# Layer 0's experts: the square root of a sum of squares on ScalarE instead of a power on GpSimd

## The reference, cut to what matters

```python
V = x @ Wv.T + bv                                   # after a layer norm of x
r = Vf @ Wg.T + bg                                  # [tokens, 8]
pv = einsum('epd,nd->nep', Wp, Vf)                  # [tokens, 8 experts, 8 projections]
c = sqrt(sum(pv * pv, axis=-1)) / sqrt(8)           # [tokens, 8]
s = _ln(r, g_r, b_r) + sigmoid(alpha) * _ln(c, g_c, b_c)
topv, sel = top_k(s, 2)
w = softmax(topv, axis=-1)
for e in range(8):
    h = silu(Vf @ W1[e].T + b1[e])
    out = h @ W2[e].T + b2[e]
    we = sum(where(sel == e, w, 0.0), axis=-1)
    delta = delta + out * we[:, None]
return Vf + delta                                   # added to x
```

## Time and profile before

| | before |
|---|---|
| median of 3 runs | 1920.31 us (1911.11 to 1921.92) |
| profiled execution | 1911.35 us |
| its span, first to last instruction | 1909.3 us |
| mean granted TensorE clock | 0.935 of 2.4 GHz |
| busy: PE / DVE / ACT / POOL | 1602.4 / 1267.7 / 1025.7 / 791.0 us |
| table loads on ACT | 13 |
| chain that ended last | PE 58%, DVE 20%, ACT 11%, POOL 6% |

### The profile page before, as it was taken

How to read it: one execution, slowest core, us unless ns; L and a number is a source line. 1 busy time by engine, 2 the same in 40 slices (tenths; PEclk the granted TensorE clock), 3 DMA queues, 4 the chain that set the end, 5 groups by cost and what they waited for, 6 DMA issues and landing times.

```text
span 1909.3 us, 29013 instructions
## 1 busy us (share of the span) xinstructions
PE 1602.4 (84%) x10660; PEld 920.5 (48%) x10660; DVE 1267.7 (66%) x2849; ACT 1025.7 (54%) x1967; POOL 791.0 (41%) x734
## 2 busy tenths in 40 slices
PE   6789899867988898987787889996778898999867
PEld 3456664313545676521354567651235456754214
DVE  4655558998554464799865455589975545549995
ACT  4555446655555444665455544466545554455654
POOL 2331215885132112588614220268841422117791
PEclk9999999888999998988899999998789999999789
DMA  6004402020000440212000053021100014302110
GB/s 220 1 1 137 133 16 73 28 89 12 12 1 1 141 134 11 73 40 78 12 12 1 4 162 113 14 71 59 55 12 6 1 40 135 111 18 77 49 46 12
DMA packets 91982, 105.41 MB, mean 55 GB/s; under 512 B 7104, under 2 KB 70336, under 8 KB 91584
## 3 DMA queue, kind: packets, MB, share of 16 engines
q1 hardware_dynamic: 89792, 99.37, 16.9%
q0 software_dynamic: 2048, 4.20, 0.7%
HBM read 80.60 MB, written 22.94 MB: 54 GB/s over the span
## 4 chain that ended last, share of the span: by engine, by line
PE 58%; DVE 20%; ACT 11%; POOL 6%; issue 4%; DMA 1%; DVEq 0%; SPq 0%; ACTq 0%; POOLq 0%
PE P L238 12%; DVE M L2038 7%; PE P L1652 6%; PE P L1881 4%; POOL M L2108 3%; PE P L1233 2%; PE P L406 2%; PE P L978 2%; PE P L2166 2%; DVE st L185 2%; PE P L1238 2%; PE P L1249 2%; DVE M L200 1%; PE P L1660 1%; PE P L1205 1%
## 5 line engine op out<-in xcount | busy, mean ns | idle before, releaser
L2038 DVE TENSOR_TENSOR_SCAN M<-P,M 128x512 f32<-128x512 f32 x384 | 444.9, 1204 | 19.5 <-ACT P L1973 17.8
L1973 ACT ACTIVATE P<-M,negA 128x512 f32<-128x512 f32 x384 | 262.3, 689 | 170.5 <-DVE M L2038 167.9
L1881 PE MATMUL P<-M,wt 32*32 32x512 f32 x3072 | 247.0, 712 | 105.4 <-DVE M L2038 64.3
L238 PEld LDWEIGHTS P<-wt,M 128*128 128x128 f32 x2176 | 278.2, 194 | 100.5 <-issue 43.9
L238 PE MATMUL P<-wt,M 128*128 128x128 f32 x2176 | 292.1, 280 | 10.0 <-ACT M L1980 4.0
L2108 POOL TENSOR_TENSOR M<-M 128x512 f32<-128x512 f32 x192 | 238.6, 1273 | 104.6 <-ACT M L1955 75.0
L2108 POOL TENSOR_TENSOR M<-W,M 128x512 f32<-128x512 f32 x192 | 242.9, 1294 | 62.9 <-PE P L1881 62.8
L1881 PEld LDWEIGHTS P<-M,wt 32*32 32x32 f32 x3072 | 38.9, 111 | 251.1 <-DVE M L2038 156.0
L1749 DVE TENSOR_TENSOR M<-M,P 128x512 f32<-128x512 f32 x128 | 87.0, 682 | 76.7 <-PE P L1660 72.5
L1652 PE MATMUL P<-M,wt 128*128 128x512 f32 x256 | 134.5, 607 | 0.8 <-ACT M L1701 0.5
L1701 ACT ACTIVATE M<-P 128x512 f32<-128x512 f32 x128 | 76.4, 597 | 101.2 <-PE P L1652 92.9
(11 more groups left out here) (352 smaller groups left out, 3225.9 us busy)
## 6 DMA issues: line engine op xcount, KB each, us to landing
W<-in_e SPq DMA_DIRECT2D x88, 192.0 KB, 2.7
M<-in_e SPq DMA_DIRECT2D x64, 192.0 KB, 2.6
M<-dt SPq DMA_DIRECT2D x48, 256.0 KB, 4.4
M<-xs SPq DMA_DIRECT2D x32, 256.0 KB, 3.2
ys<-M SPq DMA_DIRECT2D x32, 256.0 KB, 2.3
W<-du SPq DMA_DIRECT2D x32, 256.0 KB, 4.8
W<-xh SPq DMA_DIRECT2D x16, 256.0 KB
M<-du SPq DMA_DIRECT2D x16, 256.0 KB, 4.2
```

The lines of the kernel that those rows point to most:

```text
L238: m = e.matmul(out[:, tok(j)], h[:, tok(j)], wgt, start=first and j == 0, stop=last, skip_group_check=True)
L1881: m = e.matmul(t["sums"][i // 2][to:to + 32, :], part("WC", c)[r, r], scan[r, :], start=c == 0, stop=c == 5, tile_position=(32 * i, to))
L1973: e.activation(t["aa"][n % 2][:, :], t["dtr"][i][:, :], EXP, scale=negA[:, c:c + 1]).then_inc(ACT.s, ACT.mark(b, "a3", "aa", n))
L2038: e.tensor_tensor_scan(bb[:, :], t["aa"][n % 2][:, :], bb[:, :], 0.0, MUL, ADD).then_inc(DVE.s, DVE.mark(b, "a3", "scan", n))
```

## The change

ScalarE's own square root, with its scale of 1/8 applied to the input, takes the place of VectorE's multiplication and GpSimd's power. It stands in ScalarE's queue after the square and ahead of the hidden layer's identity and tanh. The sums now wait in `sm[:, 72:104]` for ScalarE and the roots go to the same place as before, `sm[:, 40:72]`; VectorE's next step waits for ScalarE instead of GpSimd.

```diff
+    SQRT = ACTF.Sqrt
@@ act_ffn0
                 ACT.s, ACT.mark(b, "f0", "sq"))
+            yield
+            w.wait_ge(DVE.s, DVE.of(b, "f0", "c0"))
+            e.activation(sm[:, 40:72], sm[:, 72:104], SQRT, scale=0.125).then_inc(ACT.s, ACT.mark(b, "f0", "c"))
             for c in range(2):
@@ dve_ffn0
                 DVE.s, DVE.mark(b, "f0", "c0"))
-            yield
-            w.wait_ge(DVE.s, DVE.of(b, "f0", "c0"))
-            e.tensor_scalar(sm[:, 72:104], sm[:, 72:104], 0.125, None, MUL).then_inc(DVE.s, DVE.mark(b, "f0", "c1"))
@@ dve_ffn0
-            w.wait_ge(POOL.s, POOL.of(b, "f0", "c"))
+            w.wait_ge(ACT.s, ACT.of(b, "f0", "c"))
@@ pool_ffn0
-            yield
-            w.wait_ge(DVE.s, DVE.of(b, "f0", "c1"))
-            e.tensor_tensor(sm[:, 40:72], sm[:, 72:104], wv("phalf"), POW).then_inc(POOL.s, POOL.mark(b, "f0", "c"))
@@ TURNS
-            "scalar": (1644,
-                "002400333318e7ff69df001089009bb2fe7f7b44217503374ae88087d9884491949249a4a040244adfaffbfffffdb6f76961"
+            "scalar": (1652,
+                "0000600da71a39ffb4edb002224026d9bebb3111adee052dcee68101f662451412a2495511021112b7f3fffbfffedb7eb4aa"
...
```

More of the change, by code:

```diff
@@ L2266, in program @@
             "tensor": (2211,
[L2267 to L2270, removed]
@@ L2271, in program @@
-                "0b584c95ff07b201b33e800366436ffc2d77fffe07f0800001089840ef0c70ffe237bb3ccd140f7fe10fe1be136e80000000"
-                "3cf003e1ed519feeeeeefdddee87a576ac12bffffff08f8506dfe"),
-            "scalar": (1644,
-                "002400333318e7ff69df001089009bb2fe7f7b44217503374ae88087d9884491949249a4a040244adfaffbfffffdb6f76961"
[L2275 to L2285, removed]
@@ L2286, in program @@
-            "gpsimd": (682,
-                "01fc1c1fc0de0e0e0000000702400fffffffcffd7f0cff003ff031e38e00000004c90003fffffefbfcffc33fc1c1fc0de0e3"
-                "40000002320400fffffff6ff5ff0cff0707f037838b00000004c90003fffffffffffccc"),
+                "000000400b10ab7ff0a77ffff50fe0800002113083ae18e1ffc46ec708618dfff381f83e1e7bce40000000000dbc3d7b28f7"
+                "f3bbbf7f9b77c1e93bc03d7f85ac248dff03d01010f10fc400ee09fdfffff6c3f83d3040000093c1ebffa38f0ffc4f368907"
+                "863bfe01e0fe136e8000003cf06800b86d493f776f77b7777bc1e93bc017ff06b84c93ff07950079be8003d907db7c2cf7ff"
@@ new lines, in program @@
+                "fe0ef08000024780f24bb7fe18e8fe22f461080f7fc30f92f0cd772000001e780d481fe0bbde27f777777eec007a565a0f91"
+                "ae0619f0afe64007aa03c67c807e11fbfffff6c3f83d3008000024f07c36fef3f3dd9e662108717fe10f92fe136e80000000"
+                "0006fc3d7549fd76bbf7777ff741e93bc03d7ffffff08f8a1e67e"),
+            "scalar": (1652,
+                "0000600da71a39ffb4edb002224026d9bebb3111adee052dcee68101f662451412a2495511021112b7f3fffbfffedb7eb4aa"
+                "48b04133f016ca53fef6b552e60102915efd37f5fa2446580b3b4b680afc34b04481249126249041112b7f3fdfffffaafef7"
+                "55448b1ff80217271bd19ff4b7b004148912ef74dfafa0812ea066d35b409fa6dd208580a4924a000010885ffff7feeafdea"
+                "5a5fdeb0998123be16d253fef6b552c9802124abcfdfbdfa0842ea067b4b68081de621124651111924a841112b7f3fffbfff"
+                "fffffe8d888ff"),
@@ new lines, in program @@
+            "vector": (2239,
+                "0000003fceb0a03be000000536fc00d9fffebfcafe080600001222403ffe80fffbfd31481e141701fc804034fff15ff32492"
+                "49489317d2a0005e3feffff555faad03bff8007b07800fffff0807c6ff4000000246ff3ff5f7bfbff82c0210404103d4ff0f"
+                "affffc06806486140c0bf5778005f9fdd4c90649124992fa540005e1f57ffabffaad03bffe5007707b7980ffffccf40e8000"
+                "06503fa01dd7fff779eff000580400800fc3b73ffffa06d186036014c07f2f3ccfa02bfec5a924924cb8080295000ebd557f"
+                "d5681dfff55503df06aaa0ffff57e807c6ff400000001eff3dbefddfff6c900c008821439c3f93ffffb40d186486140c0bf4"
+                "0012afff0bff44445124aad2fa540005e3fefffffffffff986aa01ffe07e"),
@@ L2289, in program @@
+            "gpsimd": (674,
+                "01fc383f019e38380000000709003fffffff3ffcfc33f181ff037838e00000001309003fffffefbfd7fc33fc383f03783f00"
+                "0000100050903ffdfbfcffff63cff181ff03783838000000130a003fffffffffffccc"),
             "sync": (191,
```

## The result

The changed kernel takes 1975.78 us (median of 4 runs, 1971.82 to 1987.89), the kernel before 1917.83 us beside it (1911.11 to 1921.92): a ratio of 1.0316 (95% interval 1.026 to 1.0373), 58 us or 3.2% slower. The forecast was 1935 us in a range of 1911 to 1952: right in its sign, and too low by 41 us. The profiled run took 1973.61 us, for a span of 1971.2.

The account below looks back on a forecast made before the run. It took ACT's chain of waits in the f0 stages as the path there, PE in block 3. Loads and roots 19.4 us, less credits 3.0 and 1.4, gave 15.0 on 1920.3: 1935 us, own range 1925 to 1945, whole 1911 to 1952.

Parts of the forecast that it names:

- the rest of the order is also written anew: Whole program's rewritten order, which the earlier trace can't price; put between 9.5 us gained and the same lost.
- the power's removal: Eight POOL powers and eight DVE multiplications in f0, off the chain; removal costed at nothing, gain at most 9.5 us.
- the sign of this failure: If stages outside f0 differ by more than some microseconds, the rewritten order has decided, not the table loads.
- Loads on the path as summed: Main case: loads and roots on ACT's path in the eight f0 stages, 19.4 us before credits; chance 0.59.
- block 3, put at 1.0: In block 3's f0 PE is the path, so loads and root cost 1.0 us out of 0 to 2.8.
- The even stages were to be 2 to 3 us longer each: Expected in the profile after: four even f0 stages each 2 to 3 us longer, other stages as before.
- The wait for the reduction: In f0 the root waits for DVE's 0.42 us reduction; the 1.28 us load ahead of it covers that.
- The credits, 3.0 + 1.4 us: Earlier router result lets PE's last part of f0 start sooner: 3.0 us in block 6, 1.4 in block 3.
- a switch holds ACT for its load and no longer: Each load on ACT in f0 priced at 1283 ns; the rival of dearer switches, 1946 or 1957 us, had chance 0.07.
- loads that are hidden: Rival: PE works through f0's loads, so little or nothing changes, 1920 to 1926 us; chance 0.22.
- a router that comes earlier: Rival: PE's end of f0 starts up to 4.6 us sooner per block, in full -17 us, 1903; chance 0.12.
- The chance of "slower": Whole kernel slower beyond the 9.6 us a measurement can tell, covering the forecast and the dearer switch: 0.66.

Follow-up runs that it names:

- e3: The changed kernel in its new order, with a scaled copy in the square root's place and no added table loads; 1950.45 us, ratio 1.0166.
- e10: The changed kernel's code in the order of before, with a copy in the square root's place and no added loads; 1926.73 us, ratio 1.0053.
- after: The changed kernel itself, in its new order with root and loads, against the kernel before; 1975.78 us, ratio 1.0316.
- e2: The whole change, root and loads, but every instruction kept in the order of before; 1956.73 us, ratio 1.0199.
- e5: e1 with two more PE products per block ahead of the second hidden product, results unused; 1940.67 us, ratio 1.0122.
- e1: The kernel before, power and order kept, with only the sixteen table loads added; 1952.95 us, ratio 1.0190.
- g3: e9 with two more PE products per block ahead of the second hidden product; 1940.95 us, ratio 1.0122.
- e9: e2 with the root's table load moved behind the eviction of V in seven of eight blocks; 1949.04 us, ratio 1.0151.
- g4: e2 with the square root moved behind the second tanh; 1950.47 us, ratio 1.0162.
- f1: The changed kernel with two more PE products per block ahead of the second hidden product; 1961.38 us, ratio 1.0234.
- g1: The kernel before with two more PE products per block ahead of the second hidden product; 1929.20 us, ratio 1.0050.
- e8: The kernel before with two 512-column ACT copies into unused tiles where each load would stand, no loads; 1941.22 us, ratio 1.0129.
- h2: e10 with the new order between the f0 stages only, copy for the root, no added loads; 1958.16 us, ratio 1.0216.
- h4: e10 with the new order only in a1 to f3 of blocks 4 and 5; 1945.46 us, ratio 1.0127.

## Why the prediction was wrong, step by step

**The step that failed first: "the rest of the order is also written anew ... I put its effect between the 9.5 us that the power's removal could at most give and the same amount lost."** It costs 22 us (e3 less e10, after less e2). The bound had no ground: the waits for the power say nothing about where a merge of two lanes over some 2200 turns of PE places a3's scans. The prediction named the sign of this failure itself, stages outside f0 that differ by more than some microseconds, and they do by 21. Rows like those of DVE in a3 of blocks 4 and 5 are where an unknown order shows; before it runs, only a far wider bound was honest. The order could have been read there too: it moves instructions in stages that have nothing to do with the change.

**The second, as large: the "Loads on the path as summed", 19.4 us for loads and roots.** The mechanism was right, the size was 38 us (e2; 10 for a root without loads, 28 for the loads on top). The price of a load, 1283 ns, was right, and so was the chain. Two things were missing. The sixteen loads seem to cost about their full length, 20.5 us, in every block: e5 still loses 23 us with most of the low clock gone, and block 3, put at 1.0 because PE is the path there, is 4.9 us longer in e1. And the sum left out what PE does meanwhile, 12 us by e5. It took a stall at its length, with PE's work behind it as long as before; PE waits about 3 us in one piece, and the work behind the wait then runs at 1.2 GHz. The even stages were to be 2 to 3 us longer each and are 7.5, of which 2.5 are there without loads too (e3). The earlier trace rows showed a clock of 1.00, and I took it as given rather than as something that PE's steady work kept up. The Trainium skill ("TensorE: Matmul & The Clock Gate", HAM oscillation — how this bites in real kernels) describes waits between bursts of matmuls after which the next burst runs at half clock, with DMAs as what PE waits for; the traces agree with the pattern (0.50 behind 3.40 us of waiting, 1.00 behind 1.33), with ACT as what PE waits for. No rival was built from it.

**The wait for the reduction, which "the load of 1.28 that stands ahead of the root covers".** With the loads, so it is (e2 and e1 agree). Without them the root's place costs 10 us (e10): what a load covers in the sum is not free, it is only counted once.

**The credits, 3.0 + 1.4 us, for the router's result being earlier.** No run isolates them. Block 6, for which most was credited, has the longest even stage of all after, 44 us by windows, at a clock of 0.74.

**What held.** No run shows a gain from the power's removal; the loads do stand on the chain; a switch holds ACT for its load and no longer; the rivals of loads that are hidden and of a router that comes earlier are refuted by the time. The chance of "slower" was 0.66, and the sign came out for one of two reasons of like size, the other being the order, which the prediction held as likely to help as to harm. The range ended 24 us short, because a term that no row could price was given a narrow bound and PE's clock behind a stall no term at all. (The upper end of the forecast's own range, 1945, is not the 1920.3 + 22.4 = 1943 that the prediction names for it, but 1935 + 9.5; this changes nothing.)

No version run here beats the kernel before. The best with a root on ACT is g3 at 1940.95 us, 1.2% behind it.

## What to carry to other kernels

A stall that reaches PE is not priced by its length alone: look at the clock in the stage, and where a few microseconds of waiting fall in one piece (2.5 to 4.0 us here), reckon with work behind it at half speed. A function that needs another table set is best tried where its engine feeds nobody, a place that no run here had; in a stage in which ACT evicts for PE throughout, moving it about mostly changed who waits (e9, g4). And where a change comes with a newly laid out order, price the order by itself, by running it with the change's cost taken out, before the change is judged.

## What the runs showed that was not expected

- Sixteen more matmul products made two kernels with loads faster, by 12 us (e5) and 14 us (f1), and the kernel before slower by 10 (g1).
- Waits of 3.06 us (e1, block 2), 3.40 us (after, block 6) and 3.59 us (g4, block 0) were followed by stretches at a granted clock of 0.53, 0.50 and 0.50; behind the 1.33 us of e5 it was 1.00.
- Two copies of 17 us in all, with no load, cost 25 us at the place of the loads (e8): it takes no switch of tables to lose more than ACT's own time there.
- A piece of an order brings its waits with it: 7.59 and 11.33 us in the changed kernel, in e3, in h2 and in h4, whatever ran before it.
